# Eight steps for four in a turn of the attention loops of a decoder layer

## What is computed

```python
def reference(x, ctx_1024, L0_attn_w_qkv, L0_attn_w_out, ...):
    x = x + _L0_attn_ref(_layernorm(x), L0_attn_w_qkv, L0_attn_w_out)       # 16 heads of 8, rotary, window 32
    x = x + _L0_xattn_ref(_layernorm(x), ctx_1024, L0_xattn_Wq, ...)        # 16 heads of 8, window 16
    x = x + _L0_ffn_ref(_layernorm(x), L0_ffn_gate_w, L0_ffn_w1, L0_ffn_w2) # top 2 of 8 experts, 128 -> 512 -> 128
    return x
```

## Time and profile before

| | us |
|---|---|
| median of 3 runs | 567.29 |
| lowest and highest | 566.72, 568.52 |
| span of the profiled execution | 562.7 |

### The profile page before, as it was taken

One profiled execution on the slowest core, in us unless ns is written; L12 is line 12 of the kernel. 1 busy time (PEld: TensorE's weight loads), 2 busy tenths in 40 slices (PEclk: granted clock), 3 DMA queues, 4 the chain that ended last, 5 costly groups with the idle time before them and its releaser, 6 DMA issues.

```text
span 562.7 us, 30637 instructions
## 1 busy us (share of the span) xinstructions
PE 485.7 (86%) x11903; PEld 400.6 (71%) x11903; DVE 372.7 (66%) x1314; ACT 332.5 (59%) x985; POOL 308.3 (55%) x413
## 2 busy tenths in 40 slices
PE   2689999999999798898999999973799999999930
PEld 2367777777776566676777777751599999999920
DVE  5467888888877355677877777665166666666626
ACT  3367778777786576787888887852134343343400
POOL 2444455445536343577778786767055555555624
PEclk9999999999999898999999999985799999999985
DMA  8211111111110000011111111012222222222139
GB/s 234 77 57 50 47 57 56 48 50 51 56 58 23 13 17 13 23 48 31 38 33 38 33 41 37 28 36 85 48 68 72 67 64 71 65 67 72 48 138 322
DMA packets 40801, 34.93 MB, mean 62 GB/s; under 512 B 6413, under 2 KB 37263, under 8 KB 40736
## 3 DMA queue, kind: packets, MB, share of 16 engines
q1 hardware_dynamic: 24752, 19.62, 11.1%
q0 software_dynamic: 4320, 8.53, 4.6%
q10 hardware_dynamic: 11664, 5.88, 4.4%
HBM read 18.58 MB, written 11.68 MB: 54 GB/s over the span
## 4 chain that ended last, share of the span: by engine, by line
PE 79%; issue 6%; DVE 4%; DMA 3%; SPq 2%; POOL 2%; ACT 1%; ACTq 1%; DVEq 0%; POOLq 0%
PE p_scores L1029 11%; PE p_probsT L533 11%; PE p_att_bank L523 8%; PE p_scores L416 8%; PE p_att_bank L1038 6%; PE p_v_bank L1038 5%; PE p_scores L461 4%; PE p_v_bank L486 4%; PE p_scores L409 4%; PE p_att_bank L471 3%; PE p_qk L437 2%; PE p_qk L428 2%; PE p_v_bank L502 2%; PE p_att_bank L820 2%; SPq L330 2%
## 5 line engine op out<-in xcount | busy, mean ns | idle before, releaser
L662 POOL TENSOR_TENSOR k_heads<-qk,consts 128x512 f32<-128x512 f32 x64 | 66.8, 1044 | 99.8 <-DVE qk L724 58.2
L1114 POOL DMA_INDIRECT expert_results<-weighted,result_at x71 | 75.5, 1063 | 71.5 <-DVE weighted L1102 49.1
L737 DVE TENSOR_REDUCE shift<-p_scores 128x8 bf16<-128x512 f32 (+1 forms) x128 | 74.1, 619 | 24.0 <-PE p_scores L416 23.5
L1078 ACT ACTIVATE hidden<-p_scores 128x512 f32<-128x512 f32 x71 | 42.4, 597 | 78.9 <-PE p_scores L1029 58.7
L560 ACT COPY probsT<-p_probsT 128x512 f32<-128x512 f32 x128 | 75.6, 590 | 21.1 <-PE p_probsT L533 21.0
L533 PE MATMUL p_probsT<-consts,probs 128*128 128x128 f32 x512 | 80.0, 280 | 0.4
L566 ACT ACTIVATE probs<-p_scores 128x512 f32<-128x512 f32 x128 | 78.0, 610 | 0.3 <-PE p_scores L461 0.3
L1029 PE MATMUL p_scores<-gotT,w_now 128*128 128x128 f32 x568 | 76.7, 279 | 1.6 <-ACT gotT L1081 1.6
L878 POOL DMA_INDIRECT sent_rows<-row,slot_u x64 | 64.3, 1005 | 15.8 <-issue 15.8
L1029 PEld LDWEIGHTS p_scores<-gotT,w_now 128*128 128x128 f32 x568 | 70.5, 195 | 1.8 <-ACT gotT L1081 1.8
L619 ACT COPY values<-p_v_bank 32x128 f32<-32x128 f32 x256 | 68.4, 267 | 2.2
(11 more groups left out here) (133 smaller groups left out, 951.6 us busy)
## 6 DMA issues: line engine op xcount, KB each, us to landing
got<-sent_rows ACTq DMA_DIRECT2D x71, 66.0 KB, 1.9
swapped<-raw SPq DMA_DIRECT2D x64, 64.0 KB, 1.9
w<-w_in SPq DMA_DIRECT2D x32, 128.0 KB, 2.3
back<-expert_results SPq DMA_DIRECT2D x8, 512.0 KB, 6.6
ctxT<-ctxT_in SPq DMA_DIRECT2D x32, 64.0 KB, 1.9
out<-x SPq DMA_DIRECT2D x8, 256.0 KB, 5.2
x<-x_in SPq DMA_DIRECT2D x4, 448.0 KB, 9.8
expert_results<-weighted,result_at POOLq DMA_INDIRECT x71, 2.4
```

Of the source, the lines that this page charges most:

```text
L662: nc.gpsimd.tensor_tensor(k_heads[:, :, BLK:], qk[:, 1:2, :].to_broadcast([P, G, P]), cv(C_HEAD, G).unsqueeze(2).to_broadcast([P, G, P]), ...
L737: nc.vector.tensor_reduce(shift[:, half * 8:half * 8 + 8], p_scores[:, half * 8:half * 8 + 8, low:WIN], AX.X, ALU.max).then_inc(s_max, 1)
L1114: nc.gpsimd.indirect_dma_start(out=results, out_offset=bass.IndirectOffsetOnAxis(ap=result_at[:, slot:slot + 1], axis=0), in_=weighted[:, ...
```

## The change

TURN becomes 8. The loops cover the same steps: 2 to 25 in 3 turns of eight, 8 to 23 in 2 turns of eight, and the straight steps before and after are the same ones. Two waits had the number of counts in a turn written out as 32 (for four tiles); it becomes `8 * TURN`. All other values already follow from TURN.

```diff
@@ -259,7 +259,7 @@
         FIRST = -5
         SELF_FIRST = -6
-        TURN = 4
+        TURN = 8
         LOOP_FROM = (2, 8)
@@ -852,7 +852,7 @@
                 if not isinstance(h, int) or c - 4 >= 4:
-                    nc.scalar.wait_ge(s_sent[t], 32 * h + 32 * ((c - 4) // 4))
+                    nc.scalar.wait_ge(s_sent[t], 8 * TURN * h + 32 * ((c - 4) // 4))
@@ -933,7 +933,7 @@
                     for t in range(half.start, half.stop):
-                        V.wait_ge(s_sent[t], 32 * h + 32 * ((c - 5) // 4))
+                        V.wait_ge(s_sent[t], 8 * TURN * h + 32 * ((c - 5) // 4))
```

## The result

The change costs 36 us: 603.46 us in the median (600.89 to 609.43) for 567.26, a ratio of 1.065 with a 95% interval of 1.059 to 1.070. The forecast was 600. The profiled execution is the slowest of the four; its span is 607.5 us for 562.7. In the executions for which both were recorded, the time lies 1.8 to 2.9 us over the span. So 607.5 belongs to an execution 6 us slower than the median after, and 562.7, which lies 4.6 under the median before, to one some 2 to 3 us faster than that median; the two spans differ by 44.8 us where the medians differ by 36.2.

What follows compares the result with a forecast made beforehand. TensorE was taken to bound the kernel; turn ends -2.9, streaming +14.6 and +3.0, jumps +14.4 and clock +3.7 sum to +32.8 us, so 567.3 becomes 600 us, range 581 to 614.

Steps and rivals of the forecast that it cites:

- What bounds the kernel: Whole kernel: TensorE, busy 86% of the span with 79% of the chain; its losses in the attention loops are the kernel's.
- rival A: TensorE's loops: the doubled code stays and only the longer first turns are streamed, +1.0, 568.3 us; chance 5%.
- B: TensorE's loops: code stays and the first turns' added fetches hide, only turn ends count, -2.9, 564.4 us; chance 3%.
- (2) Fewer turn ends: Both loops: three turn ends go in the first and two in the second, -2.9 us.
- (3) Streaming: Both loops: every turn fetches all its TensorE code, +14.6 us (0.73 a step) and +3.0 (0.25 a step).
- (4) Jumps: Three branches back miss their target's block and then the next, 2 x 2.4 us each, +14.4; bounds +7.2 and +25.5.
- (5) Clock: At the three jump edges idle time brings the clock down, 1.2 us a fall, +3.7; bounds 0 and +8.5.
- case of 588 to 612 us: Whole kernel: the forecast case, spanned by the bounds of (3) to (5); chance 68%.
- C: TensorE's loops: blocks are fetched again ahead of need and only the jumps back miss, 578.8 us; chance 6%.
- D: Jumps back: streaming as forecast, but the branch's target is fetched in good time, +14.7, 582 us; chance 8%.
- E: Loops and edges: everything at its dear end, jumps of 8.5 us and seven clock falls, 616 us; chance 10%.
- (6) The other engines: Other engines' doubled code: a miss hides under TensorE's, nothing, at most 2.4 us at one edge.

Runs made afterwards that it cites:

- pe_turn4: Changed kernel with TensorE alone kept at turns of four steps, the other engines at eight: 563.71 us for 564.93 before, ratio 0.996.
- pe_turn8: Kernel before with TensorE alone in turns of eight steps, the other engines in turns of four: 596.86 us, ratio 1.061.
- pe8_head0: TensorE alone in turns of eight, its two loops begun at the first instruction of a 16 KB block: 586.36 us, ratio 1.041.
- pe_straight: Kernel before with TensorE's loops in both attention stages written out as straight code, other engines in turns of four: 589.88 us, ratio 1.045.
- pe4_head0: Kernel before with TensorE's two loops begun at the first instruction of a 16 KB block: 565.32 us, ratio 1.005.

## Why the prediction was right

**What bounds the kernel** held: the loss is TensorE's, by pe_turn4 and pe_turn8, and rival A's and B's condition (the doubled code stays) is excluded by 95 packets where "some 90" was said and 57 would have meant A or B.

**(2) Fewer turn ends, -2.9**, can't be seen apart from the rest. It stands in the sum as it was.

**(3) Streaming, +17.6.** The price is nearly right within the changed kernel. In the first loop, away from the two edges, 20 steps take:

```profile
35.74:76.82 41.08, 36.50 (x1148) 27.17 (x1149) 28.54 (x70) 27.25 (x80) 16.84 (x28) 0.96 0.16 49
149.54:189.21 39.67, 36.23 (x1148) 27.36 (x1149) 28.42 (x71) 26.58 (x78) 16.37 (x27) 0.96 0.16 49
```

With the six of 96.01 to 129.47 us that is 114.2 us, 5.71 a step, 0.87 over 4.84. The six alone, in which the clock never fell, have 0.74, where 0.73 was taken from the earlier trace rows; in the other two stretches one step each ran partly at the lower clock and took 7.9 us. In the kernel without loops the same steps cost 1.1. The first turn of four steps, from which I read the price, is a short sample for a cost that comes in lumps of 1 to 2 us, wherever a block ends, and sometimes brings the clock down. In the second stage 0.25 was taken; 0.29 was measured in the changed kernel (14 steps in 81.4 us) and 0.33 in the one without loops.

**(4) Jumps, +14.4** for three, 4.8 each in two equal parts. The two parts are there, for the reason given (pe8_head0 removes the second), but the first is 4.3 to 4.9 us and not 2.4. The 2.4 was the time from the start of one packet to the resumption, and this is the term that was mis-sized most. In the first branch (81.6 to 86.1 us) two packets start, as in the second; in the third it is one. The DMA view of the first:

```profile
q8 instruction: 2, 0.03, 4.3%
```

One of them is likely the block past the loop's end, fetched ahead for nothing, which I had put into the high end alone (1.3 us); no run separates the two. An edge's idle time is 6.2 to 7.3 us, 20.6 for the three, where 14.4 was forecast.

**(5) Clock, +3.7.** Three falls at the edges, as forecast, but of 10.2 us each, not of 3.4. The two steps around each jump:

```profile
76.82:96.01 19.19, 11.99 (x334) 9.06 (x329) 7.83 (x20) 7.00 (x20) 4.91 (x9) 0.73 0.12 34
129.47:149.54 20.07, 12.77 (x333) 9.63 (x330) 7.83 (x20) 7.28 (x21) 5.61 (x10) 0.74 0.11 32
313.19:333.74 20.55, 14.32 (x347) 10.87 (x341) 9.40 (x45) 9.78 (x32) 10.27 (x14) 0.75 0.10 31
```

Two resident steps take 2 x 4.84 = 9.7 us in the first stage and 22.09 / 2 = 11.0 in the second. So the three edges cost 9.5, 10.4 and 9.5 us over resident steps. Six streamed steps lie in them, whose own price belongs to (3); without it (2 x 0.87 or 2 x 0.29) the edges cost 7.8, 8.7 and 8.9 us, where 4.8 + 1.2 was forecast. Some 5 of these 25 us are more than the idle time, and the clock is the only other cause seen for them; 3.7 was forecast for it.

So (4) and (5) together were sized too low, 18.1 us for 25 measured, and streaming with the turn ends too low by 2: the loops of the profiled execution grew by 42.3 us, where 32.8 was forecast. That the median came out only 3.5 us above the forecast does not bear the sizes out, for the medians compare an execution after that is 6 us faster than the profiled one with one before that is 2 to 3 us slower. The prediction's case of 588 to 612 us does not follow from its own bounds either: those of (3) to (5), added up, give 578 to 630. And the kernels with and without loops divide the loss otherwise than the prediction: streaming alone cost 25 us (pe_straight), where 12.7 to 18 was expected, and the three jumps added to it 596.86 - 589.88 = 7.0 us, where (4) and (5) had 18.1, for the straight run has late blocks and falls of the clock of its own in those steps. The mechanism was right; that the sum came so near was in part luck.

The signs given in advance came true: turns of 45 us plus about 5 (50.8, 52.7 and 49.9 us), idle pieces of 2.0 to 4.9 us at or just behind the first mask matmuls, and a clock of 0.50 beside them.

Of the rivals, C (streaming hidden) is refuted by pe_straight, which streams without a jump and loses 25 us; D (the target fetched in good time) by the branch rows; E's jumps of 8.5 us of idle time did not come (6.2 to 7.3), but with the clock counted an edge cost as much.

**(6) The other engines**: nothing, as said. q14 has 23 packets for 19 in the changed kernel and in pe_turn4, which lost nothing.

What stays open: why straight code pays 1.1 us a step where the turns of eight pay 0.87 (0.78 in pe_turn8). A part of it is the clock: in pe_straight three of the 24 steps ran partly or mostly at the lower level, of which two are shown here, against two of 20 in the turns of eight:

```profile
74.55:82.73 8.18, 6.37 (x170) 4.88 (x164) 3.52 (x10) 4.00 (x13) 3.24 (x6) 0.79 0.14 44
119.81:127.22 7.41, 7.41 (x169) 5.76 (x165) 3.52 (x10) 3.05 (x9) 2.32 (x5) 0.57 0.12 38
```

The rest is that the late blocks stop TensorE for longer: its idle pieces of 0.5 us or more come to 0.69 us a step in pe_straight and to 0.46 in the turns of eight, away from the edges. No run shows why. The turns repeat one layout of blocks three times, while a straight run samples many, and no run varied the layout inside the turns alone.

## What to carry to other kernels

Before more steps are put into a loop's turn, count its instructions on each engine and compare with the largest body that the instruction queue's packets show to be kept; with 1,348 TensorE instructions in a turn there was room for a quarter more (1,732, with the loop begun at a block's start), not for double. Look for instruction packets inside a loop's later turns and for branches of microseconds: either one says that the body no longer fits. If one engine is at its limit, give it its own, shorter turn; the engines need not turn together as long as they meet on semaphores.

## What the runs showed of the hardware

- TensorE keeps a body of 1,732 instructions (6.8 packets of 16 KB) from turn to turn and refetches one of 1,988 (7.8) completely: 47 packets for 93.
- A jump to a block that isn't held stops TensorE for 3.6 to 5.0 us; a second stop of 2.0 to 2.6 us follows if the target lies near its block's end. A jump ahead of a loop to the start of a block took 0.4 to 2.6 us (pe8_head0, pe4_head0).
- Code that is only streamed costs too: 0.7 to 1.1 us per step of some 337 instructions where TensorE otherwise takes 4.84 us for them, and 0.3 where a step takes 5.5.
- At each of the three edges the clock fell to its lower level for 10.2 us. After single late blocks it sometimes fell for 3.4 us (1.86 us idle, from 192.4 us before the change) and sometimes not (36.09 us in pe_straight, 1.58 us idle, clock 1.00).
- A hint for the branch shortens it (1.4 to 3.2 us for 3.7 to 4.8) and is followed by 2.7 to 3.7 us of idle time where the loop is left.
